# Two transformer blocks on one core: GpSimd applies the norms that VectorE applied, and steps move

## What is computed

```python
def _ln(x):
    mu = jnp.mean(x, axis=-1, keepdims=True)
    var = jnp.var(x, axis=-1, keepdims=True)
    return (x - mu) * jax.lax.rsqrt(var + LN_EPS)
...
x_norm = modulate(_ln(x), shift_a, scale_a)
qkv = x_norm @ W_qkv + b_qkv
...
attn_w = jax.nn.softmax(jnp.einsum('bhqd,bhkd->bhqk', q, k) * scale, axis=-1)
x = x + gate_a[:, None] * attn_out
q_c = _ln(x) @ W_qc + b_qc
kv_c = _ln(context) @ W_kvc + b_kvc
...
x = x + c_attn_out
x_norm2 = modulate(_ln(x), shift_m, scale_m)
h = jax.nn.gelu(x_norm2 @ W_mlp1 + b_mlp1)
```

## Time and profile before

| | |
|---|---|
| time, median of 3 runs | 498.83 us (498.73 to 499.41) |
| profiled execution | 499.31 us, its span 497.5 us |
| TensorE busy | 428.4 us, 86% |
| VectorE busy | 351.3 us, 71% |
| ScalarE busy | 289.2 us, 58% |
| GpSimd busy | 61.4 us, 12% |
| VectorE, applying the norms (L584) | 112 instructions in 28 groups of four |

### The profile page before, as it was taken

How to read it: one execution, slowest core, us unless ns; L and a number is a source line. 1 busy time by engine, 2 the same in 40 slices (tenths; PEclk the granted TensorE clock), 3 DMA queues, 4 the chain that set the end, 5 groups by cost and what they waited for, 6 DMA issues and landing times.

```text
span 497.5 us, 10420 instructions
## 1 busy us (share of the span) xinstructions
PE 428.4 (86%) x3664; PEld 271.1 (54%) x3664; DVE 351.3 (71%) x938; ACT 289.2 (58%) x535; POOL 61.4 (12%) x74
## 2 busy tenths in 40 slices
PE   0466699999999989889979989999999998989886
PEld 0433355656666664555545545656566665746464
DVE  4979477888888973875966948997979895531331
ACT  1022177666666666476665575656566667677552
POOL 5711010103021210210011001010101102020130
PEclk9989599999999999999999999999999999999989
DMA  8727475552746543323425136256546463510001
GB/s 256 268 64 212 146 218 138 175 138 84 195 162 171 164 131 107 92 80 113 96 83 165 42 118 152 81 154 194 135 147 154 137 184 113 116 38 24 1 1 42
DMA packets 34410, 63.30 MB, mean 127 GB/s; under 512 B 5535, under 2 KB 9887, under 8 KB 34079
## 3 DMA queue, kind: packets, MB, share of 16 engines
q1 hardware_dynamic: 34071, 62.42, 43.7%
q10 hardware_dynamic: 288, 0.21, 0.1%
HBM read 31.81 MB, written 26.74 MB: 118 GB/s over the span
## 4 chain that ended last, share of the span: by engine, by line
PE 61%; DVE 21%; DMA 5%; issue 4%; ACT 3%; POOL 3%; SPq 2%; DVEq 0%; ACTq 0%
PE ps_max L910 10%; PE ps_ao L942 9%; PE ps_sc L930 9%; PE ps_misc L892 8%; DVE maxima L680 7%; PE ps_misc L987 5%; PE ps_misc L967 5%; PE ps_misc L950 4%; DVE xn L584 4%; PE ps_misc L854 4%; DVE stats L574 3%; PE ps_misc L973 3%; POOL rstd L739 2%; DMA Kd<-Kh 2%; PE ps_misc L899 2%
## 5 line engine op out<-in xcount | busy, mean ns | idle before, releaser
L680 DVE TENSOR_REDUCE maxima<-ps_max 128x4 f32<-128x512 f32 (+1 forms) x256 | 159.7, 665 | 54.7 <-PE ps_max L910 47.4
L824 ACT ACTIVATE PT<-ps_sc 128x512 f32<-128x512 f32 (+1 forms) x256 | 138.9, 596 | 66.9 <-PE ps_sc L930 65.3
L910 PE MATMUL ps_max<-Kd,Qh 128*128 128x512 f32 (+1 forms) x256 | 105.1, 479 | 15.0 <-DMA Kd<-Kh 9.7
L930 PE MATMUL ps_sc<-Qd,Ks 97*128 97x512 f32 (+1 forms) x256 | 93.5, 444 | 0.9 <-issue 0.9
L942 PE MATMUL ps_ao<-PT,V 120*9 120x128 f32 (+1 forms) x2048 | 80.0, 274 | 0.3
L910 PEld LDWEIGHTS ps_max<-Kd,Qh 128*128 128x128 f32 x256 | 44.5, 195 | 51.5 <-issue 19.6
L942 PEld LDWEIGHTS ps_ao<-PT,V 120*9 120x9 f32 (+1 forms) x2048 | 43.3, 90 | 38.2 <-issue 33.5
L736 POOL TENSOR_SCALAR vareps<-mv 128x4 f32<-128x4 f32 (+1 forms) x28 | 6.4, 229 | 414.8 <-DVE mv L577 414.8
L930 PEld LDWEIGHTS ps_sc<-Qd,Ks 97*128 97x128 f32 (+1 forms) x256 | 44.5, 187 | 17.1 <-issue 9.9
L811 ACT ACTIVATE xnT<-ps_misc,vec 128x128 f32<-128x128 f32 x80 | 30.1, 460 | 35.2 <-PE ps_misc L854 18.8
L892 PE MATMUL ps_misc<-xnT,W 128*128 128x512 f32 x72 | 37.8, 639 | 6.4 <-ACT xnT L811 6.4
(11 more groups left out here) (74 smaller groups left out, 441.6 us busy)
## 6 DMA issues: line engine op xcount, KB each, us to landing
Qd<-q_mem SPq DMA_DIRECT2D x128, 96.0 KB
k_mem<-Kh SPq DMA_DIRECT2D x16, 512.0 KB, 2.9
q_mem<-Qh SPq DMA_DIRECT2D x16, 512.0 KB, 2.9
Ks<-k_mem SPq DMA_DIRECT2D x8, 768.0 KB, 7.1
Ks<-k_mem SPq DMA_DIRECT2D x8, 720.0 KB, 6.6
k_mem<-Kl SPq DMA_DIRECT2D x16, 256.0 KB, 3.2
q_mem<-Ql SPq DMA_DIRECT2D x16, 256.0 KB, 3.3
Kd<-Kh SPq DMA_DIRECT2D x128, 16.0 KB
```

The costliest lines, as they stand in the source:

```text
L680: dve.tensor_reduce(dst, ps_max[:, st.k % MAX_BANKS, 0:HG * ns].rearrange("p (h k) -> p h k", h=HG), AX_X, ALU.max, negate=True).then_inc( ...
L824: act.activation(PT[0:ns, st.k % 4, :], ps_sc[0:ns, st.k % 2, :], ACT.Exp, scale=SCALE).then_inc(S["probs_ready"], 1)
L910: pe.matmul(ps_max[:, st.k % MAX_BANKS, 0:HG * ns], Qh[:, st.f % 2, st.b * P:(st.b + 1) * P], Kd[:, HG * st.n:HG * st.n + HG, st.b * ns:(s ...
L930: pe.matmul(ps_sc[0:ns, st.k % 2, :], Ks[:, st.f % 2, st.n, st.b * ns:(st.b + 1) * ns], Qd[:, half % 3, st.n % GP, :, st.b * P:(st.b + 1) ...
```

## The change

The function `norm` moves from VectorE to GpSimd: the same four tensor_scalar, now behind GpSimd's own power. VectorE keeps `statistics`. Before it overwrites `mv` it now waits until the previous norm has been applied, since another engine reads it. In the first unit GpSimd applies the norm ahead of the clearing of Qd; before, the clearing came right behind the power. The order in VectorE's queue loses all xn and cn rows. And 35 due times in T and one in EARLY are different, which moves steps on all engines.

```diff
-    cln=(-36.36, -36.97, -39.16, -35.75),
-    cT=(-37.74, -34.54, -37.66, -34.98),
+    cln=(-35.96, -41.61, -38.76, -35.48),
+    cT=(-38.82, -37.61, -38.74, -36.06),
...
-                def statistics(src, rows, which):
+                def statistics(src, rows, which, before):
...
                     linked()
+                    if before:
+                        dve.wait_ge(S["cn_ready" if which else "xn_ready"], CB * before)
                     for b in range(CB):
                         dve.bn_aggr(mv[0:rows, which, b, :],
                                     stats[0:rows, which, b, :]).then_inc(S["var_ready"], 1)
...
+                def norm(src, rows, dst, which, rstd_no, ready):
+
+                    pool.wait_ge(S["rstd_ready"], rstd_no)
+                    for b in range(CB):
+                        pool.tensor_scalar(dst[0:rows, b, :], src[0:rows, b, :], mv[0:rows, which, b, 0:1],
+                                          rstd[0:rows, which, b:b + 1], ALU.subtract,
+                                          ALU.mult).then_inc(ready, 1)
...
                         pool.tensor_tensor(rstd[0:rows, which, :], vareps[0:rows, which, :],
                                            minus_half[0:rows, :], ALU.pow).then_inc(S["rstd_ready"], 1)
-                        if st.norm_no == 0:
+                    elif st.kind == "ln":
+                        if st.k:
+                            pool.wait_ge(S["misc_filled"], xT_use[st.k - 1] + 1)
+                        norm(x[:, st.s, :, :], P, xn, 0, st.norm_no + 1, S["xn_ready"])
+                        if st.k == 0:
 
                             fill(2, f32(Qd[0:SROWS, 0, :, :, :]), 0.0)
                             fill(3, f32(Ks[SROWS:SROWS + 1, :, :, :]), 1.0)
                             fill(4, f32(Qd[0:SROWS, 1, :, :, :]), 0.0)
                             fill(5, f32(Qd[0:SROWS, 2, :, :, :]), 0.0)
+                    elif st.kind == "cln":
+                        if st.k:
+                            pool.wait_ge(S["cnT_ready"], st.k)
+                        norm(craw[:, st.s, :, :], NS_CTX, cn, 1, st.norm_no + 1, S["cn_ready"])
```

More of the change, by code:

```diff
@@ L142 @@
     ln=(-41.92, -32.45, -34.0, -33.49),
-    xT=(-33.75, -29.85, -31.0, -31.32),
+    xT=(-33.38, -29.89, -31.0, -31.32),
     k=(-30.64, -29.8, -29.79, -30.79),
     q=(-28.32, -28.33, -28.43, -29.07),
-    v=(-24.95, -25.93, -25.56, -27.01),
+    v=(-24.93, -26.53, -26.02, -27.07),
     kmask=(-29.06, -28.9, -28.9, -29.9),
     kstep=(1.17, 1.64, 2.89, 2.2),
-    max=(-25.18, -24.3, -24.3, -23.5),
+    max=(-25.18, -24.3, -24.64, -23.5),
     mstep=(1.05, 0.98, 1.05, 0.9),
-    mT=(-8.4, -8.35, -8.63, -7.91),
+    mT=(-8.4, -8.35, -8.66, -7.91),
     kload=(-17.38, -19.64, -16.62, -18.08),
     qload=(-15.04, -14.45, -15.14, -18.02),
-    mload=(-9.4, -7.28, -7.49, -7.87),
+    mload=(-9.4, -8.51, -7.49, -8.19),
     copy=(0.74, 0.68, 0.5, 0.73),
[L156 to L159, removed]
+    norm=(4.0, 2.14, 3.14, 2.9),
+    aT=(4.67, 3.8, 5.0, 4.06),
+    o=(5.55, 4.65, 11.98, 5.49),
+    yT=(8.08, 9.99, 6.9, 10.05),
     mln=(6.75, 7.66),
@@ L163 @@
     mh2=(11.23, 14.05),
-    myT=(12.15, 14.13),
+    myT=(11.84, 14.13),
     bias=(-7.72, -11.42, -11.72, -11.32),
     apply=(1.7, 5.52, 1.8, 0.95),
-    kstore=(1.02, 2.25, -0.06, 0.1),
-    qstore=(0.68, 4.8, 7.11, -0.75),
-    mstore=(-2.11, -0.79, -0.31, -3.32),
+    kstore=(1.02, 2.25, -0.03, 0.1),
+    qstore=(-0.14, 3.98, 6.29, -1.57),
+    mstore=(-2.11, -0.79, -0.31, -3.53),
     msecond=(1.18, 0.88, 0.88, 7.04),
@@ L172 @@
     klo=(1.7, 1.3, 6.22, 3.35),
[L173 to L176, removed]
-    cln=(-36.36, -36.97, -39.16, -35.75),
-    cT=(-37.74, -34.54, -37.66, -34.98),
+    qlo=(1.3, 0.36, 3.52, 1.8),
+    khi=(0.63, 0.34, -0.19, 1.16),
+    qhi=(-0.15, 0.2, 2.42, 1.19),
+    value=(2.15, 2.16, 2.15, 2.55),
+    cln=(-35.96, -41.61, -38.76, -35.48),
+    cT=(-38.82, -37.61, -38.74, -36.06),
     mapply=(1.37, 0.87),
 )
-EARLY = [-0.6, 1.18, 0.4, 0]
+EARLY = [-0.6, 0.2, 0.4, 0]
 MLP_LATER = {6: 11.9}
@@ L578, in statistics @@
                                     stats[0:rows, which, b, :]).then_inc(S["var_ready"], 1)
[L580 to L586, removed]
                 def rope(st):
@@ L645, in _ @@
                             dve.wait_ge(S[f"x_in{st.s}"], 16)
-                        statistics(x[:, st.s, :, :], P, 0)
+                        statistics(x[:, st.s, :, :], P, 0, st.k)
                         if st.k == 0:
@@ L650, in _ @@
                         dve.wait_ge(S["ctx_in"], 16)
[L651 to L665, removed]
+                        statistics(craw[:, st.s, :, :], NS_CTX, 1, st.k)
+                    elif st.kind == "ln" and st.k == 0:
+                        for g in range(2):
+                            dve.memset(f32(Kd[:, g * GH:(g + 1) * GH, :]), 0.0).then_inc(S["zeros_ready"], 1)
+                            if g == 0:
+                                modulation()
                     elif st.kind in ("k", "q") and ATTN[st.a]["rope"]:
```

## The result

The changed kernel takes 535.38 us (median of 4 runs, 534.31 to 537.75) where the kernel before, beside it, took 499.12. The ratio is 1.072 (95% interval 1.0667 to 1.0775): 36 us slower. The forecast was 488.3 us, its range 482 to 494.5. Sign and size are wrong, and all rivals are passed, the slower one of 503 us too.

What follows compares the result with a forecast made beforehand. TensorE was taken as the fullest engine, busy 428.4 us or 86% of the span, with a start of chained waits. Terms -8.2 - 0.6 + 5.0 - 1.7 - 2.0 - 3.0 = -10.5 us gave 488.3 us, range 482 to 494.5.

Steps and rivals of the forecast that it cites:

- Part 1: Start: GpSimd norms stream 0 ahead of its clears, so VectorE's silu and vec finish sooner; minus 8.2 us.
- The second branch: Start: silu still waits for a whole clear, vec ends at 20.8, and 3.9 us of gain are left.
- the first branch: Start: silu waits for one norm instruction, not for a clear; vec ends at 16.5, 8.2 us earlier.
- Part 2: First unit, SyncE's queue: Kd for unit 1 issued ahead of its stores of K; minus 0.6 us, at most 3.
- the moved steps: v, yT and pairs of maxima run earlier; add and remove nothing on TensorE, priced at 0, 2 us either way.
- the cn waits: TensorE's 4 waits for cn, 2.0 us in all; moving the cn norms 4.6 steps forward removes them, -2.0.
- Part 3: Norms on GpSimd: 0.42 us an instruction, +0.5 us per norm at ten places, +5.0, against -1.7 and -2.0.
- My own break-even: Norm price that uses up the -15.5 us of the other terms: 1.55 us per norm, 0.69 us an instruction.
- rival 3: Norms: GpSimd's tensor_scalar with pointer operands far dearer; at 0.8 us an instruction 503 us, slower than before; chance 0.05.
- The bias collision: At two norms (202.1 and 479.5) GpSimd's bias add held VectorE's norm; on one engine this goes, -1.7.
- Part 4: VectorE gives up 96 + 16 instructions, 31 us, so TensorE waits less for maxima; -3 us (0 to -9).
- Rival 1: Last two attentions: GpSimd's norms and VectorE's rope sums hold one another, eight norms wait 0.7 us, +5.6, 494 us; chance 0.20.

Runs made afterwards that it cites:

- the new order: Kernel before with the changed kernel's due times, norms on VectorE: 495.28 us, ratio 0.9904; with GpSimd's clears behind the first norm as well: 487.57 us.
- the clears alone: Kernel before, norms on VectorE, one added wait: GpSimd clears Qd and Ks only after the first norm is applied; 493.23 us, ratio 0.9876.
- the short norm: Changed kernel, but GpSimd's norm writes one sequence whole and 16 columns of a second, the rest zero; 484.53 us, ratio 0.970.
- the two-input form: Changed kernel with the whole norm as two two-input tensor_tensor instructions over all four sequences on GpSimd; 508.56 us, ratio 1.018.
- The split norm: Changed kernel, but VectorE applies three sequences of each norm and GpSimd one, the first norm whole on GpSimd; 483.01 us, ratio 0.9674.
- the kernel with 64 columns: Changed kernel, but GpSimd norms only 64 of the 128 columns of each sequence, the rest zero; 507.50 us, ratio 1.018.

## Why the prediction was wrong, point by point

**Part 1, the start: right.** Forecast -8.2, measured 8.5 at the first Kd transfer and 8.8 at the first score. It reached the end of the kernel: 487.57 against 495.28 in the new order (-7.7), and a ratio of 0.9876, -6.2, in the old. The mechanism is the one told, shown by moving the clears alone. The second branch (silu behind a whole clear) did not come, and silu didn't even wait for an instruction of the norm, as the first branch had it. The norm's 3.13 us instead of 1.68 did no harm here, as TensorE's modulation products and vec lie over it.

**Part 2 and the moved steps: right in sign, too small.** Together with the cn waits they were -2.6; the order alone measured -4.8 (-6.5 to -3.1 by the interval). Part 2 by itself fits in size: the new order brings the first score from 61.85 to 61.41, and with the clears behind the norm from 54.47 to 53.98, 0.4 to 0.5 us where 0.6 were forecast. The cn waits went as said. Of what was priced 0, the wait ahead of the transposed maxima fell from 4.5 to 1.7 us. The step said that moved steps add and remove nothing on TensorE; they removed waits.

**Part 3, the norm: this step failed, three times over.** First its price. I bounded a GpSimd tensor_scalar by a clear and a two-input add and took 0.42 us; it takes 0.79. Neither row has pointers, and neither has the operation of one input and two steps; that no row showed it was known, and the range went only from one neighbour to the other. My own break-even was 0.69 us, and rival 3 got 0.05. The row that spoke for it, a power that takes 1.04 us on 4 elements, went into rival 3 alone. Second the places. I took the ten where TensorE already waited for xn, and left nine more, "hidden" by maxima and scores, to the range at the small price; there are 13 more. With a norm 2 us longer all sixteen behind 170 us wait, the ten and six of the hidden ones; the seven hidden ones before 170 us stay hidden. The cover was too short, as at 171.33, where it was a pair of maxima and two scores, 1.1 us. The count of waits in a trace says which covers are used up by the present length, not by a longer one. Third, the price of a wait. I let a wait cost its own length; here 29.9 us of longer waits brought 21.8 us of slower matmuls. At the right length and the ten places alone a norm on the path costs 3.13 - 1.12 - 0.1 = 1.9 us instead of 0.5, and the sum would have been 14 us higher, 502 to 503: rival 3's number. The other 33 us are places and clock.

The Trainium skill, page "GPSIMD Engine Reference", section "Engine selection", gives GpSimd about half of VectorE's speed for two inputs and roughly line rate for one. Its advice to leave elementwise work on VectorE, which the prediction weighed and set aside, pointed the right way. In size the trace disagrees: the one-input norm takes 3.13 us against 1.12 on VectorE, a factor of 2.8, and the two-input form is the cheaper of the two by element.

The bias collision was rightly told: on GpSimd no bias add lies beside a norm. That is inside the 484.5 us of the short norm.

**Part 4, VectorE lighter: the size may be right, the mechanism is shown for half of it.** Forecast -3. The short norm on GpSimd (1.27 us) takes 484.5 us, and the same order with the norm on VectorE (1.12 us) 487.6, a difference of 3 with intervals (0.967 to 0.974, 0.972 to 0.981) that overlap a little. The forecast's way is that maxima come sooner. TensorE's own waits for them (ps_max and the transposed maxima) are 8.9 us before, 6.0 with the new order and the norms on VectorE, 4.4 with the short norm and 4.5 in the changed kernel: the lighter VectorE takes 1.6 us, the order the other 2.9. The kernel with the first twelve norms on GpSimd reaches 484.6 with a wait for ps_max of 4.4 us, as long as before. What makes the rest of the 3 us stays open: the clock, and with the short norm the two bias collisions that are gone, may be part of it; the runs don't separate them.

**Rival 1, the lock: real, small.** Three of the 28 norms took longer than 3.13 us (3.91, 3.95 and 3.24), 1.7 us in all, where the rival had 5.6. The timeline of one:

```profile
211.15 0.68 DVE L607 TENSOR_TENSOR Ql<-ropeA,Qh 128x512 fp32r<-128x512 f32 x1
211.20 3.91 POOL L720 TENSOR_SCALAR xn<-x,mv,rstd 128x128 f32<-128x128 f32 x4 [0.18 <-POOL rstd L733]
...
212.98 0.68 DVE L607 TENSOR_TENSOR Kl<-ropeA,Kh 128x512 fp32r<-128x512 f32 x1
```

Two of VectorE's two-input remainders lie beside this norm, and neither is slower for it. Of the norm's four instructions the one beside Ql took 1.31 us and the one beside Kl 1.07 instead of 0.79, together the 0.78 us. The page "SBUF — State Buffer", section "SBUF: two separate sides" of the Trainium skill, has that lock for two SBUF inputs against a GpSimd instruction that reads SBUF; the trace agrees here that GpSimd was held. The split norm's two tensor_scalar, one on each engine and both from SBUF to SBUF, overlapped; there no run shows an exclusive lock. Why a clear or the two-input bias add of GpSimd holds such a VectorE instruction and a tensor_scalar of GpSimd doesn't stays open.

**The sum redone.** From the forecast of 488.3 to 535.4 are 47.1 us. The forecast expected a wait for xn of about 14 us and TensorE busy about as before; measured are 39.7 us (+25.7) and 449.1 (+20.7): 46.4.

## What to carry to other kernels

Before an operation moves to an engine that has never run it in this kernel, its price is unknown however near the neighbours look: put the break-even price beside the bound, and if the two are within a factor of two, the chance of a loss is large. Count covers, not waits: for each place ask how long the operation may become before TensorE reaches it, since a 1 us norm that is hidden may be a 3 us norm that isn't. And look for the part of a change that needs none of its risk; here it was the order of the clears and the steps (487.6 us). A norm shared by both engines then gave 483.0.

## What was not expected of the hardware

GpSimd's tensor_scalar with one input and two pointer operands takes 0.79 us for 128x128 in f32, some 3.2 ns an element on 0.4 us; the pointers are 0.16 us of it. Its two-input tensor_tensor takes 1.05 us for 512 elements, 2.1 ns each, so two of them beat four of the other (2.12 against 3.13 us).

A clear on GpSimd holds VectorE's tensor_scalar from SBUF to SBUF to its end (silu 3.16 us instead of 0.17), but not one that reads PSUM (1.80 us instead of 1.67), nor VectorE's own clear of Kd, 3.47 us beside it; and VectorE's and GpSimd's tensor_scalar overlap (1.02 us for three on VectorE beside 0.87 for one on GpSimd).

Behind a wait of 2.15 us and a second of 1.09 us TensorE's granted clock went from 1.00 to 0.50 for the next 4 us, and four matmuls took 3.75 us instead of 1.95. Behind a stop of 1.39 us alone it stayed at 1.00. Over the kernel the longer waits of the changed kernel cost three fourths as much again in slower matmuls (21.8 us on 29.9), those of the kernel with 64 columns a third (5.8 on 16.9).
